# A bias ahead of a wait, a token copy ahead of a table load, and a second output buffer in a selective-scan and mixture-of-experts kernel

## The chip, the core and the metric

The kernel runs on one core of a Trainium2 chip. The metric is the time of one execution on the device, in microseconds (us). The engines are named as the profile does: PE (TensorE, matrix products), DVE (VectorE), ACT (ScalarE, activation functions), POOL (GpSimd) and SP (SyncE, which only issues transfers here). Each engine runs its own queue of instructions in order and waits on semaphores for the others.

## What is computed

The input is x of 8 batches of 512 tokens of 256 numbers. With xn the normalised x, the output is x + attention part(xn) + expert part(xn):

```python
# attention part: a selective state-space layer, 16 states per channel
x_ssm, x_gate = split(xn @ in_proj_w.T + in_proj_b)
x_conv = silu(conv4(x_ssm) + conv_b)
B, C   = split(x_conv @ bc_w.T + bc_b)
dt     = softplus(x_conv @ dt_w.T + dt_b)
h_t    = h_(t-1) * exp(dt_t * A) + dt_t * B_t * x_t      # scan over 512 tokens
y      = (sum over states of h_t * C_t + x_t * D) * silu(x_gate)
attn   = layernorm(y @ out_w.T + out_b + xn) * ln_g + ln_b
# expert part: 8 experts, the best 2 for each token
logits = silu(xn @ rw1 + rb1) @ rw2 + rb2
w      = softmax over the two largest logits
ffn    = xn + sum over the 2 experts of w_e * (silu(xn @ we1[e] + be1[e]) @ we2[e] + be2[e])
```

## The kernel before

A first block normalises x, writes the residual and computes the router's logits. A table of 71 tiles of 128 token slots is then made, each tile belonging to one expert. The main block interleaves two jobs. For each of 8 batches `b` it runs steps `i` of 0 to 8, and each step works on one expert tile `s = 9 b + i` and, in the first eight steps, on two of the sixteen states (`g = 16 b + 2 i + r`).

*The scan.* For each state DVE multiplies by B (L920), scans (L927) and multiplies by C into a ring of four (L934). POOL adds the ring into `y` (L593). ACT makes the decays `exp(dt * A)` (L757, `decay`), two instructions for each state, up to four states ahead. For the next batch the work is spread over the steps: PE projects (`proj_in`, `proj_bc`, `proj_dt`, L1126), ACT evicts (`conv_in`, `conv_act`, `bc_in`, `dt_in`), DVE applies three taps per half (L901, in steps 2 and 3), SP stores B and C to DRAM behind the loads of step 5 (L528), and ACT's `dt_in` of step 6 waits for that store. `exp_dt` and `ln_dt` follow in steps 6 and 7. In step 8, which has no scan, DVE computes `dtt` and `u` (L909, L912), and ACT makes the first two decays of the next batch. For the batch before, `proj_out` (L1148, L1151) runs on PE in steps 8 and 0, DVE adds and takes statistics (L947, L952) in steps 0 and 1, ACT and POOL normalise in steps 3 and 4, and POOL adds into `out` (L630).

*The experts.* POOL gathers a tile's tokens (L573) three tiles ahead. PE turns them (`turn_x`, L1160) into bank `up0`, and ACT copies them to `xgt` (`copy_x`, L764). PE computes `up` in two halves, banks `up0` and `up1`: each begins with a matmul that writes the bias (L1174) and goes on with 16 matmul passes (L1180). ACT applies silu (`hidden`, L791), PE computes `down` in two halves (L1190, L1194), ACT multiplies by the row's weight into `yo` (`weigh`, L799), and POOL scatters the rows with an add into `out` (L582), each scatter after the one before has landed.

In step `s` PE does: `up` half 0 of tile s+1, a projection, `up` half 1 of s+1, `down` half 0 of s, `turn_x` of s+2, `down` half 1 of s. ACT does, in step `s`:

```python
decay(b, i + 1, 0)
table_of(ACT.Silu); hidden(s + 1, 0); hidden(s + 1, 1)
...                       # evictions of this step's projections
table_of(ACT.Exp)
copy_x(s + 2)
decay(b, i + 1, 1)        # step 8: the two first states of batch b + 1
weigh(s)
```

`table_of` (L784) runs a tiny activation, so that the load of the function's table stands there in the queue. There are no projections between `hidden` and the table load in steps 7 and 8, and in the last batch only those of steps 0 and 1.

Of the kernel before, what the change touches and what calls it, by code (L numbers as in the profile page):

```python
# [6 lines left out]
ACT = mybir.ActivationFunctionType  # L7
# [5 lines left out]
P = 128  # L13
B, L, D = 8, 512, 256
# [9 lines left out]
MT = TOPK * TOK // P + E - 1  # L24
# [3 lines left out]
PARTS = 96  # L28
# [29 lines left out]
def build(nc, x, cols, rows, wmix, wroute, brows, we1, we2, consts, constb, out):  # L58
    ctx = ExitStack()
    with ctx:  # L60
        def sb(name, shape, dt=F32):
            return ctx.enter_context(nc.sbuf_tensor(name, shape, dt))

        def sem(name):
            return ctx.enter_context(nc.semaphore(name))

        psum = {n: ctx.enter_context(nc.psum_tensor("ps_" + n, [P, 512], F32))
                for n in ("up0", "up1", "yx", "fr")}
# [17 lines left out]
        sel = sb("sel", [PARTS, 32], BF16)  # L86
# [3 lines left out]
        sid = sb("sid", [P, MC], I32)  # L90
        wslot = sb("wslot", [P, MC])
# [19 lines left out]
        th = rep[:, 1, :, :].rearrange("p r l -> p (r l)")  # L111
        ht = sb("ht", [P, HBUF, KH, P])
        bup = bpart[:, 0:H].rearrange("p (e c) -> p e c", c=P)
        yo = sb("yo", [P, D])

        rt_i = sb("rt_i", [P, TB], I32)
        scrap = sb("scrap", [P, 4])
# [352 lines left out]
        s_hidden = sem("s_hidden")  # L470
        s_down_ready = sem("s_down_ready")
        s_weighed = sem("s_weighed")
        s_scattered = sem("s_scattered")
# [5 lines left out]
        yx_y, tr_x = psum["yx"][:, 0:D], psum["up0"][:, 0:D]  # L479
# [13 lines left out]
        def positive(n):  # L493
            return not isinstance(n, int) or n > 0

        with nc.Block() as block:
# [71 lines left out]
            def _(pool):  # L568
# [7 lines left out]
                def scatter(s, b, i):  # L576
                    if s > 0:
                        pool.wait_ge(s_scattered, s * 16)
                    if i == 5:
                        pool.wait_ge(s_out_rows, (b + B) * 16)  # L580
                    pool.wait_ge(s_weighed, s + 1)
                    pool.indirect_dma_start(out[:, :], bass.IndirectOffsetOnAxis(ap=sid[:, s:s + 1], axis=0), yo[:, :], None,  # L582
                                            bounds_check=TOK - 1, oob_is_err=False,
                                            compute_op=ALU.add).then_inc(s_scattered, 16)

# [94 lines left out]
            def _(act):  # L680
# [79 lines left out]
                def copy_x(j):  # L760
                    act.wait_ge(s_x_turned, j + 1)
                    if positive(j):
                        act.wait_ge(s_up_ready, j * 2)
                    act.activation(xgt[:, :, :], tr_x.rearrange("p (k c) -> p k c", k=KD), ACT.Copy).then_inc(s_x_copied, 1)  # L764
# [14 lines left out]
                def table_of(func):  # L779

                    n = tables[0]
                    if n >= 4:
                        act.wait_ge(s_table, n - 3)
                    act.activation(scrap[:, n % 4:n % 4 + 1], col[:, 0:1], func).then_inc(s_table, 1)  # L784
                    tables[0] += 1
# [8 lines left out]

                def weigh(j):
                    act.wait_ge(s_down_ready, j + 1)
                    if positive(j):
                        act.wait_ge(s_scattered, j * 16)
                    act.activation(yo[:, :], yx_y, ACT.Copy, scale=wslot[:, bass.ds(j, 1)]).then_inc(s_weighed, 1)  # L799

                def seed_root(b):
                    act.wait_ge(s_ln_eps, b + 1)
                    act.activation(rt_l[:, :], mv[:, :, 1], ACT.Ln).then_inc(s_ln_log, 1)
# [11 lines left out]
                def step(b, i):  # L815
                    s = b * STEPS + i
                    prepare = b < B - 1
                    if i + 1 < IN:
                        decay(b, i + 1, 0)
                    if i == 7 and prepare:  # L820
                        ln_dt(b + 1)
                    if s + 1 < MT:
                        table_of(ACT.Silu)
                        for h in range(2):
                            hidden(s + 1, h)
                    if i in (0, 1):
                        gate_in(b, i, front["gate", b, i])
                    if i == 0 and b > 0:
                        start_sum(b)
                    if i in (2, 3) and prepare:  # L830
                        conv_in(b + 1, i - 2, front["in", b + 1, i - 2])
                    if i == 4 and prepare:
                        conv_act(b + 1)
                    if i == 5 and prepare:
                        bc_in(b + 1, front["bc", b + 1, 0])
                        dt_in(b + 1, 0, front["dt", b + 1, 0])
                    if i == 6 and prepare:
                        dt_in(b + 1, 1, front["dt", b + 1, 1])
                    if i == 3 and b > 0:
                        seed_root(b - 1)  # L840
                    table_of(ACT.Exp)
                    if i == 3 and b > 0:
                        seed_exp(b - 1)
                    if s + 2 < MT:
                        copy_x(s + 2)
                    if i + 1 < IN:
                        decay(b, i + 1, 1)
                    if i == 8 and prepare:
                        for r in range(NU):
                            decay(b + 1, 0, r)  # L850
                    if s < MT:
                        weigh(s)
                    if i == 4 and b > 0:
                        normalise(b - 1)
                    if i == 6 and prepare:
                        exp_dt(b + 1)
# [263 lines left out]
            def _(pe):  # L1120
# [44 lines left out]

                def up(b, i, e, h):
                    j, q = b * STEPS + i, i % WBUF
                    if h == 0:
                        pe.wait_ge(s_x_copied, j + 1)
                        pe.wait_ge(s_w1[q], b * (16 * STEPS // WBUF) + 16 * (i // WBUF) + 16)  # L1170
                    if positive(j):
                        pe.wait_ge(s_hidden, j * 2 - 1 + h)
                    bank = psum[f"up{h}"]
                    pe.matmul(bank[:, :], bup[:, bass.ds(e, 1), :],  # L1174
                              sel[:, 4 * h:4 * h + 4].unsqueeze(2).to_broadcast([PARTS, 4, P]),
                              start=True, stop=False)
                    for c in range(4):
                        at = (4 * h + c) * P
                        for k in range(KD):
                            mm = pe.matmul(bank[:, c * P:(c + 1) * P], w1s[:, q, k, at:at + P], xgt[:, k, :],  # L1180
                                           start=False, stop=(c == 3 and k == KD - 1))
                    mm.then_inc(s_up_ready, 1)
# [15 lines left out]
                def step(b, i, e, e_next):  # L1198
# [3 lines left out]
                    if s + 1 < MT:  # L1202
                        up(b, i + 1, e_next, 0)
# [54 lines left out]
                e = expert(0)  # L1258
# [5 lines left out]
                for b in range(B):  # L1264
                    for i in range(STEPS):
                        e, e_next = step(b, i, e, e_next)
# [62 lines left out]
```

## Time and profile before

| | |
|---|---|
| median of 3 runs | 939.42 us (939.33 to 946.33) |
| profiled execution, its own time | 945.95 us |
| its span, first to last instruction | 944.1 us |
| mean granted clock of PE | 0.948 |

The profile is of one execution. Its span is what the rows of the trace add up to; about 1.9 us lie around it. The median of the other runs is 6.5 us below the profiled one. In the rows, L757 is line 757; "x16" is a count; `[2.36 <-ACT xgt L764]` says that the engine stood idle for 2.36 us before it and what released it. A matmul's end is modelled. PEld is PE's weight load.

### The profile page before, as it was taken

To read this page: it belongs to the slowest core of one execution; us is meant where nothing else is said; L and a number is where in the kernel's file an instruction comes from. 1 tells how busy PE (TensorE), PEld (TensorE's weight loads), DVE (VectorE), ACT (ScalarE), POOL (GpSimd) and SP (SyncE) were. 2 spreads that over 40 slices of the span, in tenths; PEclk is the share of its full clock that TensorE was granted. 3 is DMA by queue.
4 is the path that set the end of the run, shared out by engine and by line. 5 is a ranking of instruction groups with operands and counts; after the bars stand their busy time and mean duration, and the time that the engine had idled before them with its cause. 6 is when DMAs were issued, how large, how long until landed. Compare 5 with 4: busy or idle time off the path is not lost.

```text
span 944.1 us, 14375 instructions
## 1 busy us (share of the span) xinstructions
PE 796.2 (84%) x4533; PEld 637.8 (68%) x4533; DVE 786.6 (83%) x772; ACT 663.5 (70%) x1132; POOL 602.8 (64%) x384
## 2 busy tenths in 40 slices
PE   3995759978997999889988999989988998899841
PEld 2671558857786777777876887677767776778731
DVE  7818677799889988998899798989897989879973
ACT  1433577867788868876887879787887688769910
POOL 3570434657477757876777756875678478759760
PEclk9996679999999999999999999999999999999975
DMA  9945584567566876696668765887588667877721
GB/s 300 375 145 172 179 292 167 166 200 251 185 206 218 249 231 192 201 290 209 204 201 254 245 222 172 244 253 221 162 230 273 208 191 209 255 230 215 213 62 23
DMA packets 81912, 201.02 MB, mean 213 GB/s; under 512 B 7920, under 2 KB 41200, under 8 KB 81712
## 3 DMA queue, kind: packets, MB, share of 16 engines
q1 hardware_dynamic: 61424, 171.46, 53.4%
q0 software_dynamic: 19152, 26.59, 14.6%
q10 hardware_dynamic: 1264, 2.05, 0.7%
q8 instruction: 40, 0.66, 0.3%
q14 instruction: 32, 0.26, 0.1%
HBM read 174.38 MB, written 26.61 MB: 213 GB/s over the span
## 4 chain that ended last, share of the span: by engine, by line
PE 33%; DVE 26%; issue 11%; ACT 10%; DMA 8%; POOL 2%; SPq 2%; DVEq 0%; POOLq 0%; ACTq 0%
PE ps_up L1180 13%; DVE ps_drive L927 10%; PE ps_yx L1194 8%; DVE ring L934 7%; PE ps_fr L1126 6%; DMA bc_scratch<-sp 5%; DVE ps_drive L920 5%; ACT L784 3%; PE ps_fr L1151 2%; ACT da L757 2%; PE ps_up L1174 2%; DVE xx L901 2%; POOL y L593 1%; SPq L520 1%; DMA out<-yo,sid 1%
## 5 line engine op out<-in xcount | busy, mean ns | idle before, releaser
L593 POOL TENSOR_TENSOR y<-y,ring 128x1024 f32<-128x1024 f32 x127 | 328.4, 2586 | 57.8 <-ACT y L748 50.7
L927 DVE TENSOR_TENSOR_SCAN ps_drive<-da,ps_drive 128x1024 f32<-128x1024 f32 x128 | 293.7, 2295 | 48.8 <-ACT da L757 45.2
L1180 PEld LDWEIGHTS ps_up<-xgt,w1s 128*128 128x128 f32 x2272 | 285.7, 197 | 18.0 <-issue 9.6
L1180 PE MATMUL ps_up<-xgt,w1s 128*128 128x128 f32 x2272 | 285.5, 280 | 0.0
L1194 PE MATMUL ps_yx<-w,ht 128*128 x1136 | 269.8, 381 | 0.0
L1194 PEld LDWEIGHTS ps_yx<-w,ht 128*128 128x128 f32 x1136 | 205.8, 191 | 28.5 <-issue 5.0
L582 POOL DMA_INDIRECT out<-yo,sid x71 | 117.3, 1652 | 144.7 <-ACT yo L799 105.2
L784 ACT ACT_TABLE_LOAD x143 | 183.5, 1283 | 2.6
L757 ACT ACTIVATE da<-gd,col 128x511 f32<-128x511 f32 x256 | 168.4, 710 | 0.0
L920 DVE TENSOR_TENSOR ps_drive<-ps_u,rep 128x1024 f32<-128x1024 f32 x128 | 157.4, 1229 | 9.7 <-DVE ring L934 0.5
L934 DVE TENSOR_TENSOR ring<-ps_drive,rep 128x1024 f32<-128x1024 f32 x128 | 156.5, 1223 | 3.9
L791 ACT ACTIVATE ht<-ps_up 128x512 f32<-128x512 f32 x142 | 81.5, 588 | 94.5 <-PE ps_up L1180 94.4
L1126 PE MATMUL ps_fr<-xx,wm 128*128 128x512 f32 (+1 forms) x224 | 115.5, 641 | 21.5 <-ACT sp L719 9.8
L1174 PE MATMUL ps_up<-sel,bpart 96*128 96x512 bf16 x142 | 55.6, 392 | 46.9 <-ACT xgt L764 32.1
L573 POOL DMA_INDIRECT xg<-xn_scratch,gid x71 | 74.7, 1052 | 29.2 <-issue 12.7
L1126 PEld LDWEIGHTS ps_fr<-xx,wm 128*128 128x128 f32 (+1 forms) x224 | 38.1, 188 | 61.0 <-issue 36.3
L901 DVE SCALAR_TENSOR_TENSOR xx<-xs,col,xx 128x512 f32<-128x512 f32 x48 | 46.2, 962 | 24.5 <-ACT xx L697 23.9
L1174 PEld LDWEIGHTS ps_up<-sel,bpart 96*128 x142 | 14.1, 99 | 75.6 <-issue 74.6
L799 ACT ACTIVATE yo<-ps_yx,wslot 128x256 f32<-128x256 f32 x71 | 32.9, 464 | 27.0 <-DMA out<-yo,sid 25.3
L1160 PE MATMUL ps_up<-ident,xg 128*128 128x128 f32 x142 | 27.6, 276 | 13.1 <-DMA xg<-xn_scratch,gid 8.3
L727 ACT ACTIVATE sp<-ps_fr,col 128x512 f32<-128x512 f32 x16 | 11.0, 687 | 38.2 <-PE ps_fr L1126 22.3
L1151 PE MATMUL ps_fr<-wm,y 128*128 128x256 f32 x128 | 35.6, 410 | 0.0
(142 smaller groups left out, 706.5 us busy)
## 6 DMA issues: line engine op xcount, KB each, us to landing
w1s<-in_we SPq DMA_DIRECT2D x71, 1024.0 KB, 7.2
rep<-bc_scratch SPq DMA_DIRECT2D x128, 512.0 KB, 4.6
w<-in_we SPq DMA_DIRECT2D x8, 1024.0 KB, 8.9
w<-in_x SPq DMA_DIRECT2D x8, 512.0 KB, 11.0
xn_scratch<-da SPq DMA_DIRECT2D x8, 512.0 KB, 7.1
xnt_scratch<-xx SPq DMA_DIRECT2D x8, 512.0 KB, 6.6
out<-w POOLq DMA_DIRECT2D x8, 512.0 KB, 6.5
xx<-xnt_scratch SPq DMA_DIRECT2D x8, 512.0 KB, 3.6
```

The source lines that it names most:

```text
L582: pool.indirect_dma_start(out[:, :], bass.IndirectOffsetOnAxis(ap=sid[:, s:s + 1], axis=0), yo[:, :], None, bounds_check=TOK - 1, oob_is_e ...
L593: pool.tensor_tensor(y[:, :, :], y[:, :, :], ring[:, g % RING, :, :], ALU.add).then_inc(s_sum, 1)
L757: act.activation(da[:, g % DECAYS, k, 1:], dtt[:, k, 1:], ACT.Exp, scale=aneg[:, k, n:n + 1]).then_inc(s_decay, 1)
L784: act.activation(scrap[:, n % 4:n % 4 + 1], col[:, 0:1], func).then_inc(s_table, 1)
L791: act.activation(ht[:, j % HBUF, 4 * h:4 * h + 4, :], psum[f"up{h}"][:, :].rearrange("p (k c) -> p k c", c=P), ACT.Silu).then_inc(s_hidden, 1)
L920: dve.tensor_tensor(drive[:, :, :], u[:, :, :], rep[:, g % REPS, 0:1, :].to_broadcast([P, KD, L]), ALU.mult).then_inc(s_times_b, 1)
L927: dve.tensor_tensor_scan(states, da[:, g % DECAYS, :, :].rearrange("p k l -> p (k l)"), states, 0.0, ALU.mult, ALU.add).then_inc(s_scanned, 1)
L934: dve.tensor_tensor(ring[:, g % RING, :, :], drive[:, :, :], rep[:, g % REPS, 1:2, :].to_broadcast([P, KD, L]), ALU.mult).then_inc(s_times ...
L1126: mm = pe.matmul(psum["fr"][0:rows_out, :], wm[:, k, at:at + rows_out], src[:, k, :], start=(k == 0), stop=(k == KD - 1))
L1174: pe.matmul(bank[:, :], bup[:, bass.ds(e, 1), :], sel[:, 4 * h:4 * h + 4].unsqueeze(2).to_broadcast([PARTS, 4, P]), start=True, stop=False)
L1180: mm = pe.matmul(bank[:, c * P:(c + 1) * P], w1s[:, q, k, at:at + P], xgt[:, k, :], start=False, stop=(c == 3 and k == KD - 1))
L1194: mm = pe.matmul(yx_y, ht[:, j % HBUF, k, :], w2[:, bass.ds(e, 1), k, :], start=False, stop=(k == KH - 1))
```

## The change

Three edits. (1) In `up`, the bias of bank `up1` is written at the very start of the tile, in front of the wait for the token copy and of half 0; the bias of `up0` stays behind that wait, since the turned tokens lie in `up0`, but stands in front of the wait for the weights. (2) In ACT's step the token copy of tile s+2 goes in front of `table_of(ACT.Exp)`. (3) `yo` gets two buffers: `weigh(j)` waits for the scatter of tile j-2 instead of j-1.

```diff
-        yo = sb("yo", [P, D])
+        yo = sb("yo", [P, 2, D])
...
-                    pool.indirect_dma_start(out[:, :], ..., yo[:, :], None,
+                    pool.indirect_dma_start(out[:, :], ..., yo[:, s % 2, :], None,
...
                 def weigh(j):
                     act.wait_ge(s_down_ready, j + 1)
-                    if positive(j):
-                        act.wait_ge(s_scattered, j * 16)
-                    act.activation(yo[:, :], yx_y, ACT.Copy, scale=wslot[:, bass.ds(j, 1)]).then_inc(s_weighed, 1)
+                    if j > 1:
+                        act.wait_ge(s_scattered, (j - 1) * 16)
+                    act.activation(yo[:, j % 2, :], yx_y, ACT.Copy, scale=wslot[:, bass.ds(j, 1)]).then_inc(s_weighed, 1)
...
+                    if s + 2 < MT:
+                        copy_x(s + 2)
                     table_of(ACT.Exp)
                     if i == 3 and b > 0:
                         seed_exp(b - 1)
-                    if s + 2 < MT:
-                        copy_x(s + 2)
                     if i + 1 < IN:
                         decay(b, i + 1, 1)
...
                 def up(b, i, e, h):
                     j, q = b * STEPS + i, i % WBUF
+                    bank = psum[f"up{h}"]
+
+                    def bias(half):
+                        if positive(j):
+                            pe.wait_ge(s_hidden, j * 2 - 1 + half)
+                        pe.matmul(psum[f"up{half}"][:, :], bup[:, bass.ds(e, 1), :],
+                                  sel[:, 4 * half:4 * half + 4].unsqueeze(2).to_broadcast([PARTS, 4, P]),
+                                  start=True, stop=False)
+
                     if h == 0:
+                        bias(1)
                         pe.wait_ge(s_x_copied, j + 1)
+                        bias(0)
                         pe.wait_ge(s_w1[q], b * (16 * STEPS // WBUF) + 16 * (i // WBUF) + 16)
-                    if positive(j):
-                        pe.wait_ge(s_hidden, j * 2 - 1 + h)
-                    bank = psum[f"up{h}"]
-                    pe.matmul(bank[:, :], bup[:, bass.ds(e, 1), :],
-                              sel[:, 4 * h:4 * h + 4].unsqueeze(2).to_broadcast([PARTS, 4, P]),
-                              start=True, stop=False)
```

## Rows read from the trace of the kernel before

**Rows 1.** The page, part 1: busy time, share of span, instructions.
```profile
PE 796.2 (84%) x4533; PEld 637.8 (68%) x4533; DVE 786.6 (83%) x772; ACT 663.5 (70%) x1132; POOL 602.8 (64%) x384
```

**Rows 2.** Chain of waits, a batch boundary: start us, us, what.
```profile
606.27 6.54 DMA bc_scratch<-sp
...
622.27 0.59 ACT ht L791
...
633.59 2.31 DVE ps_drive L927
...
639.21 0.27 PE ps_fr L1148
```

**Rows 3.** The waits: who for whom, us in total, times, longest us.
```profile
ACT yo L799 <- DMA out<-yo,sid: 25.3, 15, 5.9
PE ps_up L1174 <- ACT xgt L764: 32.1, 25, 3.3
PE ps_up L1160 <- ACT ht L791: 4.8, 6, 0.9
DVE ps_drive L927 <- ACT da L757: 45.2, 17, 7.2
DVE xx L901 <- ACT xx L697: 23.9, 9, 5.1
```

**Rows 4.** Timeline of ACT: start us, us, engine, line, operation, at two boundaries.
```profile
425.79 1.06 ACT L791 ACTIVATE ht<-ps_up 128x512 f32<-128x512 f32 x2
...
630.09 1.28 ACT L784 ACT_TABLE_LOAD   x1
...
631.53 0.38 ACT L764 ACTIVATE xgt<-ps_up 128x256 f32<-128x256 f32 x1
631.82 2.55 ACT L757 ACTIVATE da<-gd,col 128x511 f32<-128x511 f32 x4
636.18 0.47 ACT L799 ACTIVATE yo<-ps_yx,wslot 128x256 f32<-128x256 f32 x1 [1.82 <-DMA out<-yo,sid]
```

**Rows 5.** Timeline of PE, the same boundary, from step 6 on.
```profile
616.10 0.39 PE L1174 MATMUL ps_up<-sel,bpart 96*128 96x512 bf16 x1 [2.36 <-ACT xgt L764]
616.32 1.95 PE L1180 MATMUL ps_up<-xgt,w1s 128*128 128x128 f32 x16
...
623.00 0.41 PE L1160 MATMUL ps_up<-ident,xg 128*128 128x128 f32 x2 [0.88 <-ACT ht L791]
...
625.26 0.39 PE L1174 MATMUL ps_up<-sel,bpart 96*128 96x512 bf16 x1
...
631.12 0.38 PE L1160 MATMUL ps_up<-ident,xg 128*128 128x128 f32 x2
```

**Rows 6.** Timeline of PE, the boundary at 437 us.
```profile
419.61 0.39 PE L1174 MATMUL ps_up<-sel,bpart 96*128 96x512 bf16 x1 [2.37 <-ACT xgt L764]
419.83 3.48 PE L1180 MATMUL ps_up<-xgt,w1s 128*128 128x128 f32 x16
...
427.09 0.38 PE L1160 MATMUL ps_up<-ident,xg 128*128 128x128 f32 x2
...
429.04 0.38 PE L1174 MATMUL ps_up<-sel,bpart 96*128 96x512 bf16 x1
```

**Rows 7.** Windows: us, busy per engine, PE's granted clock, DMA share, GB/s.
```profile
419.50:423.00 3.50, 3.39 (x17) 3.37 (x18) 3.36 (x3) 3.48 (x5) 1.34 (x3) 0.57 0.93 322
```

**Rows 8.** Timeline of PE, the first two tiles.
```profile
138.00 0.61 PE L1174 MATMUL ps_up<-sel,bpart 96*128 96x512 bf16 x1 [0.62 <-ACT xgt L764]
...
145.84 0.39 PE L1174 MATMUL ps_up<-sel,bpart 96*128 96x512 bf16 x1 [0.83 <-ACT xgt L764]
```

**Rows 9.** Timelines of ACT and POOL in the last batch.
```profile
862.31 0.38 ACT L764 ACTIVATE xgt<-ps_up 128x256 f32<-128x256 f32 x1
...
874.50 1.61 POOL L582 DMA_INDIRECT out<-yo,sid  x1 [1.07 <-ACT yo L799]
...
904.28 0.47 ACT L799 ACTIVATE yo<-ps_yx,wslot 128x256 f32<-128x256 f32 x1 [5.90 <-DMA out<-yo,sid]
```

More of the change, by code:

```diff
@@ L581, in scatter @@
                     pool.wait_ge(s_weighed, s + 1)
-                    pool.indirect_dma_start(out[:, :], bass.IndirectOffsetOnAxis(ap=sid[:, s:s + 1], axis=0), yo[:, :], None,
+                    pool.indirect_dma_start(out[:, :], bass.IndirectOffsetOnAxis(ap=sid[:, s:s + 1], axis=0), yo[:, s % 2, :], None,
                                             bounds_check=TOK - 1, oob_is_err=False,
```

## Prediction

> **What bounds the kernel now.** I read the totals first [rows 1]: TensorE (PE) and VectorE (DVE) are both busy over 80% of the span, so neither is a bound by itself and the order of waits has to say which one counts where. Then the chain of waits in order of time, over one batch boundary (batch 4 to 5; six others repeat it, at scans 240, 339, 437, 536, 732 and 831 us) [rows 2]. The reader is to see that one loop through all engines sets the period of a batch, 98 to 99 us:
>
> - In the middle of a batch DVE sets the pace. It runs its scans without a gap until the store of B and C for the next batch is issued (606.27). Its landing lets ScalarE (ACT) run dt_in, tables, softplus and the hidden of the last-but-one tile.
> - That hidden (622.27) releases the turn of the tokens at 623.00. From there PE is without a gap worth the name: rest of down, up of the batch's last tile, half a down, next turn at 631.12 [rows 5].
> - ACT has waited for that up. It loads the exponential's table at 630.09 and decays the first state of the next batch at 631.82 [rows 4]. DVE has waited for this decay: over the span 45.2 us in 17 waits [rows 3], seven of them at boundaries.
> - The scan then releases the layer norm's first add, which releases proj_out on PE (639.21), and PE runs without a gap through two tiles to the conv projection, which ACT hands to DVE's taps (23.9 us of waits in nine, about 3 at each batch [rows 3]). Then DVE sets the pace again.
>
> So a microsecond added in front of the decay at 631.82 is paid once per boundary, seven times. What happens to PE between the taps and the store of B and C costs or brings nothing: DVE is the late one there.
>
> **Part 1, the bias of the second bank in front of the wait.** Nothing is added or removed: 71 matmuls change place. Where PE waits for the token copy (25 waits, 32.1 us [rows 3]), this one, 0.2 to 0.4 us [rows 5], is now done inside the wait. Its own wait (the hidden of that bank one tile earlier) is met, since ACT runs that hidden ahead of the copy that PE waits for. On the loop PE waits for no token copy but a short one at 625.26, so per batch only one place gains: in step 0 the bias stood behind proj_out's wait for the norm's add. There the next projection waits for DVE's second add almost as long, and I take 0.1 us per boundary: -0.7. The start is different: PE waits 0.62 and 0.83 us for the first two copies [rows 8], and from there the chain is PE's. One bias in each wait, 0.4 and 0.2 us: -0.6.
>
> **Part 2, the copy in front of the table load.** ACT does the same three things, in another order. Before, at the boundary, the load (630.09) lay beside the half down and the turn on PE, and the copy came at 631.53, just when the turn (631.12, about 0.4 us) was done; the decay came 0.29 us after the copy [rows 4, 5]. Now ACT, a strict queue, stands at the copy until the turn is done, and only then loads the table. From the copy's start to the decay's it takes: copy 0.38 (the load does not overlap it), load to the next instruction's start 1.44 less about 0.03 of wait for the turn, so 1.79 to 1.8. That is 1.5 us more than 0.29.
>
> Against it stands what PE gains. In step 6 the copy comes 1.4 us sooner, and PE starts that tile 1.6 us sooner instead of at 616.10. But the next turn already waited 0.88 us for ACT's hidden in five of the seven boundaries (623.00; the sixth such wait is in the last batch [rows 3, 5]), and that hidden sits behind a softplus and three tables on ACT. So the 1.6 us become a longer wait for the hidden, 2.5 to 2.6 us, and nothing reaches the decay. The hidden itself comes 0.12 later, for the copy no longer overlaps its neighbours. The next copy is early: turn to next bias is 2.26 us there (623.00 to 625.26) and 1.95 where no copy is waited for (427.09 to 429.04) [rows 5, 6], a gain of 0.3, net 0.15. So the decay moves by 1.5 - 0.15 = +1.36 us at five boundaries. At the other two (437 and 536) PE ran up of this tile slowly (16 matmuls 3.48 us instead of 1.95) and its turn, 427.09, waited for nothing [rows 6]. ACT's hidden for it ran from 425.79 and takes 0.59 [rows 2, 4]; with the 0.12 and 0.1 to the turn PE can start it at 426.6. So the earlier start is worth 0.47 here, and the decay moves by 1.5 - 0.47 = +1.04. Sum: 5 x 1.36 + 2 x 1.04 = +8.9.
>
> In other steps a delay of up to 1.5 us (where nothing stands between hidden and copy) falls on decays for which DVE isn't waiting: of the 17 waits, the ten away from the boundaries are three of the first batch and seven of 0.6 us in step 1, ahead of the 3 us in which DVE waits for the taps anyway. What hides it is the scan in hand, with its products before and behind. If that cover were gone, it would cost 1.5 us in about three steps of each batch, 31 us. The copy is earlier by 1.4 us in steps 2 to 4 and 6, where PE did wait for it, and all that ends in DVE's stretch. In the last batch no projections stand between hidden and copy: the copy of step 2 (862.31) was already held by the turn. Its table now pushes two decays, the next hidden and so the weighing whose end POOL waits for at 874.50 [rows 9]; from there POOL has no gap up to the last accumulation into out, which holds the end. +1.0.
>
> What does a table cost? The load is 1.28 us and the next instruction starts 1.44 us after the load starts [rows 4]. The Trainium skill (ScalarE: Activation LUTs, What ACT_TABLE_LOAD costs) gives the same 1283 ns for the load but adds a drain of about 1380 ns to every switch, 2.66 us. By that the load exposed at each boundary would cost some 1.2 us more, and the sum would be some 8.5 us higher. No drain of that size stands behind the loads of this trace.
>
> **Part 3, two buffers for weighted rows.** It takes away ACT's wait for the scatter: 15 waits, 25.3 us [rows 3]. Seven of them stand right after the boundary's decays (0.6 to 1.8 us, as at 636.18 [rows 4]). Behind them are a decay for the third scan and a hidden that waits for PE anyway, and the delay of part 2 eats up most of the wait itself. The longest two are in the tail, the first 5.9 us [rows 9]; POOL is late there, with scatters and sums queued in order, not ACT. Scatters still wait for each other. I take 0; the bound on the good side is all 25.3.
>
> **The clock of PE.** Six of the seven boundaries have a long wait for the copy of step 6. After two of them the granted clock fell to half, 1.2 GHz (0.57 mean over 419.5 to 423 [rows 7]). The wait of 2.37 us was followed by it [rows 6], the one of 2.36 [rows 5] and the longest, 3.3 [rows 3], were not, so I can't say beforehand which will be. There it cost little, for the hidden behind it was late anyway. The change shortens that wait to 1 us and makes one of 2.6 us right in front of the turn, where the loop runs through PE. A fall to half there costs 3.48 - 1.95 = 1.5 us on sixteen matmuls and 0.1 on the next, 1.6 us [rows 5, 6]. I take two of them as before: +3.3. Ends: none, and six, +9.8. The Trainium skill (TensorE: Matmul & The Clock Gate, What's actually happening) says that the throttled state is the default and activity releases it; the two falls behind waits agree.
>
> **Sum.** -0.6 -0.7 +8.9 +1.0 +0 +3.3 = +11.9 us. The profiled execution took 945.95 us (span 944.1), so it would take 957.9. It is 6.5 us above the median of the runs, 939.42; none of the terms hangs on that difference that I can see, so I add them to the median: 951.3.
>
> **Rivals.**
> - *No low clock* (0.22): the longer wait before the turn never meets a fall of the clock. 939.4 + 8.6 = 948.0, at the edge of what can be told.
> - *Every such wait meets it* (0.05): 939.4 + 8.6 + 9.8 = 957.8.
> - *The second buffer pays* (0.13): ACT's wait for the scatter after the boundary's decays, and in the tail, was on a path that the chain does not show. If all 25.3 us count, 951.3 - 25.3 = 926.0; it decides for faster from about 21 us on. For it: the waits of more than 5 us in the tail, with PE's last downs behind them. Against it: no piece of the chain is a wait of ACT's weighing for a scatter.
> - *The copy's advance reaches the decay* (0.10): not ACT's hidden but PE sets the turn at all boundaries, as it does at 437 and 536. Then 1.4 to 1.6 us of advance pay for the 1.5 of the load at each, and with the start's gain it is 939.4 - 0.6 - 0.7 - 0 to 1 = 937 to 938. Against it: five waits of 0.88 us of the turn for the hidden.
> - The forecast itself: 0.50.
>
> **How the numbers follow.** A measurement of this kernel tells about 1% from no change, so the bounds are 930.0 and 948.8. Slower: the forecast 0.50, every wait 0.05, and 0.05 of the case at 948.0: 0.60. Faster: half of the second buffer's 0.13 and a little of the copy's advance: 0.08. The same: 0.32. The range reaches down to the copy's advance and leaves out most of the second buffer's case below and the far end of the clock above, less than 2 in 10: 937 to 957. The forecast's own range is 948.8 to 955.
>
> **What would show it.** After the change: at a boundary ACT's copy stands after a wait for the turn (1 us or more), with the table load behind it, and DVE's first scan of a batch waits over 1 us longer for its decay than before, up to 8.5 where it was 7.2; L927's wait for decays grows from 45 to 55 us or more. PE's waits for the copy fall from 32 us to about half, and its waits for hidden in front of the turn grow from 4.8 to 15 or more. ACT's waits for the scatter are gone. The first tap of batch 1 comes 0.6 us sooner. Wrong, if the period between first scans does not grow by 1 us, if the decays wait in the middle of batches too (then it is dearer), or if the tail after 890 us gets shorter, which would be the second buffer's doing.

## The result, and the profile after

The changed kernel takes 963.8 us (median of 6 runs, 959.5 to 968.2), the kernel before 940.2 on the same chips (6 runs). The ratio is 1.0219, with a 95% interval of 1.0182 to 1.0255: 20.6 us slower. (The medians lie 23.6 us apart; the ratio also weighs a run of 953.3 us of the kernel before.) The prediction was 951.3, in a range of 937 to 957, and the measured time lies above that range. Its sign was right; by the ratio its sum, +11.9, was 8.7 us short.
Against [rows 1] the busy time of the page moved by 4.6 us on PE and 6.7 on DVE, and so most of the 19 us are waits. Time at half clock counts as busy:

```profile
PE 800.8 (83%) x4533; PEld 637.5 (66%) x4533; DVE 793.3 (82%) x772; ACT 666.8 (69%) x1132; POOL 603.1 (63%) x384
```

The waits of the changed kernel (who for whom, us in total, times, longest us). Its `up` is at L1173 and L1185, its `down` at L1195 and L1199.

```profile
DVE ps_drive L927 <- ACT da L757: 63.0, 17, 11.9
ACT xgt L764 <- PE ps_up L1160: 32.1, 28, 4.2
PE ps_up L1160 <- ACT ht L791: 18.3, 10, 2.7
PE ps_fr L1148 <- DVE xtok L947: 16.9, 7, 3.2
ACT yo L799 <- DMA out<-yo,sid: 6.0, 1, 6.0
PE ps_up L1173 <- ACT xgt L764: 1.7, 2, 1.0
PE ps_up L1185 <- DMA w1s<-in_we: 27.8, 14, 3.5
```

Against [rows 3]: DVE's waits for decays grew from 45.2 to 63.0 us and PE's waits for the hidden in front of the turn from 4.8 to 18.3. PE's waits for the copy (32.1) and ACT's for the scatter (25.3) are all but gone. So the three edits do what they say. What PE waited for the copy, ACT now waits for the turn (32.1), and PE waits 27.8 us for weights in front of L1185; no line of the kernel before names weights, but its bias stood behind the wait for them, and there it has 14.2 us in 8 waits without a releaser. The fourth line is the one to look at: PE's wait in front of `proj_out` for the norm's add, not among the rows of the prediction, was this before:

```profile
PE ps_fr L1148 <- DVE xtok L947: 10.5, 8, 1.7
```

**A boundary with the clock at full.** Timeline of ACT after, batch 2 to 3 (start us, us, engine, line, operation, idle before it and its releaser), to set beside [rows 4, 5]:

```profile
433.85 0.60 ACT L791 ACTIVATE ht<-ps_up 128x512 f32<-128x512 f32 x1 [1.19 <-PE ps_up L1185]
435.91 0.38 ACT L764 ACTIVATE xgt<-ps_up 128x256 f32<-128x256 f32 x1 [1.46 <-PE ps_up L1160]
436.31 1.28 ACT L784 ACT_TABLE_LOAD   x1
437.60 0.20 ACT L784 ACTIVATE scrap<-col 128x1 f32<-128x1 f32 x1
437.71 2.54 ACT L757 ACTIVATE da<-gd,col 128x511 f32<-128x511 f32 x4
```

And PE over the same stretch, the turns of steps 7 and 8:

```profile
427.67 0.41 PE L1160 MATMUL ps_up<-ident,xg 128*128 128x128 f32 x2 [1.87 <-ACT ht L791]
...
435.49 0.38 PE L1160 MATMUL ps_up<-ident,xg 128*128 128x128 f32 x2
```

ACT idles 1.46 us in front of the copy, and only then does the load begin. From PE's last turn to the first decay it is 437.71 - 435.49 = 2.22 us; before, 631.82 - 631.12 = 0.70. That is the exposed load, +1.52 us, and the same at all seven boundaries within 0.06. From step 7's turn to step 8's it is 7.82 us, before 8.12 (631.12 - 623.00): 0.30 given back, so +1.22 net. That holds at the five boundaries where the turn had waited 0.88 before. At the two where it had waited for nothing (427.09 and 525.74), turn to turn was 7.80 already, but `dt_in` (L727) to the turn was 10.68 us there and is 10.10 everywhere now: 0.56 given back in all, so +0.96 net. The hidden comes late enough to eat the rest of PE's earlier start, as the wait of 1.87 shows.

**Half clock behind step 7's turn.** Timeline of PE after, batch 4 to 5:

```profile
630.17 0.41 PE L1160 MATMUL ps_up<-ident,xg 128*128 128x128 f32 x2 [2.70 <-ACT ht L791]
630.41 2.81 PE L1199 MATMUL ps_yx<-w,ht 128*128 x8
633.02 1.06 PE L1173 MATMUL ps_up<-sel,bpart 96*128 96x512 bf16 x2
633.87 4.11 PE L1185 MATMUL ps_up<-xgt,w1s 128*128 128x128 f32 x32
...
639.66 0.38 PE L1160 MATMUL ps_up<-ident,xg 128*128 128x128 f32 x2
```

Turn to turn is 9.49 us instead of 7.82: +1.67. This happened at three boundaries (after 326.8, 527.5 and 630.2 us), each behind a wait of 2.70. A fourth wait of that size, and one of 2.53, were not followed by it.

**Half clock behind step 0's wait.** The same happens in front of `proj_out`. Timeline of PE after, in a batch with the clock at full (444.75) and in one without (649.28):

```profile
444.75 0.27 PE L1148 MATMUL ps_fr<-bpart,sel 96*128 96x256 bf16 x1 [2.40 <-DVE xtok L947]
444.86 1.03 PE L1151 MATMUL ps_fr<-wm,y 128*128 128x256 f32 x4
...
649.28 0.37 PE L1148 MATMUL ps_fr<-bpart,sel 96*128 96x256 bf16 x1 [3.17 <-DVE xtok L947]
649.45 1.91 PE L1151 MATMUL ps_fr<-wm,y 128*128 128x256 f32 x4
651.15 0.42 PE L1148 MATMUL ps_fr<-bpart,sel 96*128 96x256 bf16 x1
651.37 1.91 PE L1151 MATMUL ps_fr<-wm,y 128*128 128x256 f32 x4
653.08 2.93 PE L1185 MATMUL ps_up<-xgt,w1s 128*128 128x128 f32 x16
```

Windows of the clean boundary and of this stretch (us, busy per engine, PE's granted clock, DMA share, GB/s):

```profile
427.80:437.50 9.70, 9.70 (x63) 8.53 (x62) 6.34 (x4) 6.70 (x11) 8.94 (x5) 1.00 0.82 255
649.20:656.00 6.80, 6.72 (x27) 5.81 (x28) 6.01 (x5) 0.00 (x0) 0.00 (x0) 0.56 0.46 150
```

Timeline of DVE, the first tap (L901) of each of the two batches, whose first scans start at 439.13 and 643.65:

```profile
471.88 2.86 DVE L901 SCALAR_TENSOR_TENSOR xx<-xs,col,xx 128x512 f32<-128x512 f32 x1 [2.75 <-ACT xx L697]
...
678.90 2.87 DVE L901 SCALAR_TENSOR_TENSOR xx<-xs,col,xx 128x512 f32<-128x512 f32 x1 [2.75 <-ACT xx L697]
```

The decay is later, so the scan, DVE's work behind it and the add are later, while PE has the same work as before: its wait grew from 1.5 us to 2.4 and more. In the stretch behind the wait of 3.17 the granted clock is 0.56, near the 1.2 GHz level. It fell behind a wait of 2.83 (546.25) too, and in the batch from 751.93 behind one of 2.71 for POOL's `y` in step 8's `proj_out` (753.10), but not behind one of 2.82 (345.58). Here PE leads up to the taps: from step 0's `proj_out` to the first tap it is 27.13 us in the clean batch and 29.62 in the other, and the first tap stands 32.75 us behind the first scan in the clean batch and 35.25 in the other. (DVE's own wait, 2.75, is the same in both, because on the way its scans had stood longer for PE and for a decay.) In three batches the tap was late, by 1.16, 2.50 and 1.07 us; before in none. It is the same in all the kernels of this study: of 78 batches between the second and the eighth first scan, 14 have a late first tap (by 1.07 to 2.84 us), and exactly these 14 have half clock between their first scan and that tap.

**A chain through POOL's queue.** The batch that began at 643.65 took 108.3 us. PE waited 3.48 us for weights in it and then ran `up` at a low clock (32 passes are 3.73 us at full):

```profile
694.10 6.40 PE L1185 MATMUL ps_up<-xgt,w1s 128*128 128x128 f32 x32 [3.48 <-DMA w1s<-in_we]
```

Its chain of waits (start us, us, what):

```profile
706.95 1.61 POOL out L582
708.55 2.39 POOL y L593
710.95 2.31 POOL xtok L624
713.30 2.74 issue
716.05 11.89 DMA out<-xtok
...
728.79 0.20 POOL out L582
...
736.55 9.31 DMA out<-yo,sid
...
746.67 1.57 POOL out L582
748.24 2.38 POOL y L593
```

The scatter of step 4 left late (706.95, 63.3 us behind the first scan, where 57.5 to 58.7 is usual), the sum into `out` waited for its landing, the next scatter for the sum's (7.59 us of idle POOL), and the gathers queued behind it came late for the turns. That boundary's wait for the decay is the 11.9 of the list above.

So the trace gives, over the six batches between first scans 2 and 8, 615.3 us against 590.9: +24.4. By stretches: first scan to first tap +4.7, all of it the three late taps; first tap to `dt_in` (L727) +3.5; `dt_in` to step 8's turn +7.0; turn to first scan +9.2, the exposed load. In the third stretch, 2.3 us were given back by the order, 3 x 1.67 = 5.0 are the slow turns and 4.2 the chain's batch; with its share of the second stretch the chain comes to about 6. The rest of the second stretch, about 1.6 us over five batches, is not explained by any run. The part of the trace ahead of the six batches is 2.8 shorter (first batch's first scan at 132.51 instead of 134.78, and 0.5 of the first period), the one behind them 2.3 shorter (110.50 for 112.75).

### The profile page after: what moved, and what is told of

Read it like the earlier page. It is cut to its first block, busy times and chain, and to the rows that moved or that the text cites. A ratio compares the mean times of both kernels' runs of the same rounds, so it can differ in the third digit from the quotient of the medians.

```text
span 963.4 us, 14373 instructions
## 1 busy us (share of the span) xinstructions
PE 800.8 (83%) x4533; PEld 637.5 (66%) x4533; DVE 793.3 (82%) x772; ACT 666.8 (69%) x1132; POOL 603.1 (63%) x384
## 4 chain that ended last, share of the span: by engine, by line
PE 27%; DVE 22%; DMA 14%; issue 13%; ACT 8%; POOL 7%; SPq 0%; POOLq 0%; DVEq 0%; ACTq 0%
PE ps_up L1185 9%; PE ps_yx L1199 8%; DVE ps_drive L927 7%; DMA out<-yo,sid 7%; DVE ring L934 6%; PE ps_fr L1126 5%; DMA out<-xtok 5%; DVE ps_drive L920 4%; POOL y L593 3%; ACT L784 2%; ACT da L757 2%; DVE xx L901 2%; PE ps_fr L1151 2%; POOL xtok L624 1%; PE ps_up L1173 1%
## 5 line engine op out<-in xcount | busy, mean ns | idle before, releaser
L593 POOL TENSOR_TENSOR y<-y,ring 128x1024 f32<-128x1024 f32 x127 | 324.5, 2555 | 76.7 <-ACT y L748 64.1
L1185 PEld LDWEIGHTS ps_up<-xgt,w1s 128*128 128x128 f32 x2272 | 279.7, 198 | 58.6 <-DMA w1s<-in_we 33.7
L1185 PE MATMUL ps_up<-xgt,w1s 128*128 128x128 f32 x2272 | 283.3, 282 | 27.8 <-DMA w1s<-in_we 27.8
L1199 PE MATMUL ps_yx<-w,ht 128*128 x1136 | 271.9, 383 | 0.0
L1199 PEld LDWEIGHTS ps_yx<-w,ht 128*128 128x128 f32 x1136 | 206.7, 192 | 29.1 <-issue 5.3
L582 POOL DMA_INDIRECT out<-yo,sid x71 | 119.7, 1686 | 151.3 <-ACT yo L799 97.7
L1126 PE MATMUL ps_fr<-xx,wm 128*128 128x512 f32 (+1 forms) x224 | 113.4, 631 | 22.6 <-ACT sp L719 10.3
L901 DVE SCALAR_TENSOR_TENSOR xx<-xs,col,xx 128x512 f32<-128x512 f32 x48 | 52.6, 1095 | 24.2 <-ACT xx L697 23.6
L1160 PE MATMUL ps_up<-ident,xg 128*128 128x128 f32 x142 | 27.9, 278 | 30.7 <-ACT ht L791 18.3
L764 ACT ACTIVATE xgt<-ps_up 128x256 f32<-128x256 f32 x71 | 27.1, 382 | 33.5 <-PE ps_up L1160 32.1
L1173 PE MATMUL ps_up<-sel,bpart 96*128 96x512 bf16 x142 | 46.3, 398 | 2.8 <-ACT xgt L764 1.7
L1160 PEld LDWEIGHTS ps_up<-ident,xg 128*128 128x128 f32 x142 | 19.0, 142 | 41.5 <-issue 22.0
L1148 PE MATMUL ps_fr<-bpart,sel 96*128 96x256 bf16 x32 | 9.7, 302 | 34.7 <-DVE xtok L947 16.9
```

What stands on the lines that cost most here:

```text
L593: pool.tensor_tensor(y[:, :, :], y[:, :, :], ring[:, g % RING, :, :], ALU.add).then_inc(s_sum, 1)
L1126: mm = pe.matmul(psum["fr"][0:rows_out, :], wm[:, k, at:at + rows_out], src[:, k, :], start=(k == 0), stop=(k == KD - 1))
L1199: mm = pe.matmul(yx_y, ht[:, j % HBUF, k, :], w2[:, bass.ds(e, 1), k, :], start=False, stop=(k == KH - 1))
```

## Experiments

Eleven kernels, each in 10 runs (e2, e7 and e9 in 4, e11 in 12), beside the kernel before on the same chip (941.8 to 943.1 us there, 23 to 25 runs). Ratios have their 95% interval. "Six batches" is the time between the second and the eighth first scan of the one profiled execution; before it is 590.9, after 615.3.

| label | us | ratio | six batches |
|---|---|---|---|
| e1_bias_only | 938.7 | 0.9958 [0.9932, 0.9983] | 589.6 |
| e2_copy_only | 962.1 | 1.0225 [1.0173, 1.0277] | 606.6 |
| e3_two_yo_only | 941.0 | 0.9983 [0.9951, 1.0015] | 590.9 |
| e8_bias_and_yo | 939.3 | 0.9963 [0.9933, 0.9992] | 586.1 |
| e6_not_steps_6_8 | 942.3 | 1.0014 [0.9981, 1.0047] | 592.8 |
| e4_not_step8 | 944.4 | 1.0018 [0.9990, 1.0046] | 597.1 |
| e7_only_step8 | 960.8 | 1.0176 [1.0104, 1.0247] | 613.6 |
| e5_fill_waits | 954.9 | 1.0117 [1.0084, 1.0150] | 605.8 |
| e9_fill_step0 | 955.4 | 1.0121 [1.0078, 1.0164] | 603.9 |
| e10_step8_filled | 950.0 | 1.0083 [1.0052, 1.0115] | 599.4 |
| e11_late_softplus | 938.1 | 0.9946 [0.9921, 0.9971] | 583.1 |

### Each part alone

e1 is the kernel before with the `up` of the change, e2 with its order of copy and table, e3 with its two buffers. Each diff is the part with its number (1, 2, 3) of the diff in the section on the change.

> The kernel before with part 1 alone, the bias of the second bank ahead of the wait for the token copy. Theory (the cost is made by the copy in front of the table load): no cost here, a gain of about 1 us, 937 to 940 us, and the turn of step 7 still waits 0.9 us or so for ACT's hidden. Rival (the earlier bias lets PE run ahead and idle longer before its next wait, so that its clock falls in the places that set the end): 945 us or more, with more low stretches of the granted clock than the four of before between 238 and 831 us.

> The kernel before with part 2 alone, the token copy ahead of the exponential's table load in every step. Theory (this part makes the cost): 955 to 964 us, each boundary's turn to first scan 1.5 us longer (3.6 instead of 2.1 us), PE's wait for the hidden in step 7 over 1.8 us. Rival (the low clock needs the bias in front as well): 948 to 950 us, the seven exposed loads alone, 7 x 1.2 = 8.5 us above before, with no low stretch between the turn of step 7 and the first scan.

> The kernel before with part 3 alone, two buffers for the weighted rows. Theory: ACT's 25 us of waits for scatters go to under 7 and nothing of it reaches the end, 939 us within 0.3%. Rival (the tail, which is 2.3 us shorter after the change, is shorter because of the second buffer): 937 us, the stretch from the last batch's first scan to the end under 111 us instead of 112.8.

The whole cost is part 2's: e2 alone has the ratio of the whole change. Part 1 gains 4 us by the ratio (I had 1.3). Part 3 gives nothing that the ratio can tell, though its stretch from the last first scan to the end was 110.4 us instead of 112.8, the sign that the rival had named. From the waits of e3: ACT's wait for the scatter fell from 25.3 us to one wait in the tail, and the six batches stayed as they were:

```profile
ACT yo L799 <- DMA out<-yo,sid: 5.5, 1, 5.5
```

The same view of e2: step 0's wait had grown without the other parts:

```profile
PE ps_fr L1148 <- DVE xtok L947: 20.0, 8, 3.0
```

### Parts 1 and 3 together

The whole change without its part 2.

> The change without part 2 at all: bias ahead of the wait and two buffers for the weighted rows. Theory: the gain of the bias (0.4%) and nothing or 0.2% of the second buffer: 937 to 939 us. Rival (both together let PE run ahead of DVE into longer waits): 943 us or more.

939.3 us, the base from which part 2 is taken apart below.

### Which step's copy costs

The whole change, with the copy left behind the table load in some steps (e4: 8; e6: 6 and 8), and the kernel before with the copy moved in step 8 alone (e7). Shown for e4:

```diff
-                    if s + 2 < MT:
+                    if s + 2 < MT and i != 8:            # e6: i not in (6, 8); e7: i == 8
                         copy_x(s + 2)
                     table_of(ACT.Exp)
                     if i == 3 and b > 0:
                         seed_exp(b - 1)
+                    if s + 2 < MT and i == 8:            # e6: i in (6, 8); e7: i != 8
+                        copy_x(s + 2)
```

> The whole change, but in step 8 of each batch the token copy stays behind the table load. Theory (the load exposed at the boundary is a price of its own, 1.5 us in each of seven): turn to first scan back at 2.1 us, total 10.6 us under the change, about 953 us, the rest being low clock. Rival (the low clock is nearly all, and the load at the boundary is hidden by other waits): 961 us or more.

> The whole change, but the token copy stays behind the table load in steps 6 and 8. Theory (the early copy of step 6 only moves PE's idle time in front of step 7's turn, where the half clock falls on the loop): the turn's wait back to 0.9 us and turn to turn at 8.1 us or less at every boundary, 3 to 5 us under the variant that leaves out step 8 alone (944.4), so about 940 us. Rival (step 6's early copy is harmless, and low stretches come from somewhere else): 944 us again.

> The kernel before with one thing: in step 8 alone the token copy goes in front of the table load. Theory: 1.5 us at each of seven boundaries, and with the longer wait of PE for the norm's add in step 0 the low stretches behind it, three or so of 1 to 2.5 us each: 943 + 10.5 + 4.5 = 955 to 960 us. Rival (step 0's low clock needs PE to run ahead by the early copies): 951 to 954 us and no first tap later than 32.8 us after the first scan.

Left behind in step 8 alone, the copy gives back 19 us of the 20.6 (ratio 1.0018), and moved there alone it costs 17 (1.0176, a wide interval). One instruction in one of nine steps is the case. For e4 I had expected 953 us, 10.6 less than the change and the rest left as half clock; it was 944.4. The half clock of step 0 went with the load: with the decay on time step 0's wait was 0.4 to 1.7 us and all six taps stood at 32.75. e6 and e4 have the same ratio, where I had expected e6 to be 3 to 5 us faster, so the early copy of step 6 costs nothing that can be told, though e4's profile shows the slow turn at three boundaries and e6's at none: step 7's wait for the hidden was 2.7 us at most in e4, 1.2 in e6. In e7 the waits of step 0 were 2.9 to 3.3 us and the first tap was late in all six batches, by 1.5 to 2.8 us.

### Keeping PE's clock

e5 is the whole change with matmuls that add zeros, 8 in front of step 0's `proj_out` and 16 in front of step 7's turn. e9 has only those in step 0. e10 has part 1, the copy of step 8 alone and the filler of step 0. What is computed is the same in all three.

```diff
                     if i == 0 and b > 0:
+                        for _ in range(8):
+                            pe.matmul(psum["up1"][:, :], bup[:, bass.ds(e_next, 1), :],
+                                      sel[:, 28:32].unsqueeze(2).to_broadcast([PARTS, 4, P]),
+                                      start=False, stop=False)
                         proj_out(b - 1, 1)
...
                         down(s, e, 0)
+                        if i == 7:                       # e5 alone
+                            for _ in range(16):
+                                pe.matmul(yx_y, sel[:, 31:32].to_broadcast([PARTS, P]), bpart[:, H:BW],
+                                          start=False, stop=False)
                         if s + 2 < MT:
                             turn_x(s + 2)
```

> The whole change, and in its two long waits of PE on the loop it now multiplies by zero rows: 16 short matmuls that add zero to the half-done down in front of step 7's turn, 8 that add zero to the second up bank in front of step 0's proj_out. The result is the same numbers. Theory (beside the exposed load, 1.5 us at each boundary, the cost is the half clock that follows these waits, 3 x 1.7 behind the turn and 4.7 behind proj_out, with what the latest of them drags along): no low stretch in these places, turn of step 7 to next turn 7.8 us at every boundary, first tap 32.8 us after the first scan in every batch, 950 to 954 us. Rival (the clock is a by-product and the time goes to late decays and POOL): 960 us or more, with the periods of the batches as after the change.

> The whole change with PE's filler (8 matmuls that add zeros) only in step 0, in front of proj_out's wait for the norm's add, and none in front of step 7's turn. Theory (the half clock behind step 0's wait makes the first tap late and, in one batch, starts a chain through POOL's queue): all first taps stand 32.75 us behind the first scan, turn to turn stays 9.5 us at about three boundaries, and the time lies between that of the change (963.8) and that with both fillers (954.9), nearer to the latter: 956 to 958. Rival (step 7's half clock is what costs): the time stays at 961 to 964. Second rival (the filler itself delays the add's projection): the taps come later than 33.5 us everywhere.

> Bias ahead (part 1), the copy in front of the table load in step 8 alone, one buffer yo, and the filler in step 0. The same step-8 copy without part 1 and without filler took 960.8 us with taps late in all six batches. Theory (that cost is 1.5 us of table load at each of seven boundaries plus the half clock in step 0): with the clock held only the table load is left, 938.7 (part 1 alone) + 7 x 1.4 = 948.5 us, periods 98.5 to 99.7, taps at 32.75. Rival (the load in front of the decay costs more by another path, such as the later scans pushing every store and gather): 955 us or more with taps at 32.75.

Timeline of PE in e9, step 0 of batch 5, whose first scan is at 640.85:

```profile
643.56 1.91 PE L1211 MATMUL ps_up<-sel,bpart 96*128 96x512 bf16 x8
646.48 0.27 PE L1148 MATMUL ps_fr<-bpart,sel 96*128 96x256 bf16 x1 [1.01 <-DVE xtok L947]
646.58 1.03 PE L1151 MATMUL ps_fr<-wm,y 128*128 128x256 f32 x4
```

The add comes no sooner, PE has 1.9 us more to do, and it takes 9.2 us off the whole change (1.0219 to 1.0121; the two intervals make that good to about 5). In e5, e9 and e10 all 18 first taps of the six batches stand at 32.75. The filler was not put into the kernel before; its trace has no late tap that it could mend. e5 and e9 come out the same, so it is step 0's filler that pays; the 16 matmuls in step 7 bring nothing that can be told on top, though e5's trace has no slow turn of 9.5 us (one of 8.67, six of 7.8). e9's expected rival, that step 7's half clock costs, falls. In e9 turn to turn was 9.5 us at two of the seven boundaries, where I had expected about three.

e10 has the exposed load and, in step 0, a held clock. ACT in it, at one boundary:

```profile
537.44 0.38 ACT L764 ACTIVATE xgt<-ps_up 128x256 f32<-128x256 f32 x1 [1.46 <-PE ps_up L1162]
537.84 1.28 ACT L784 ACT_TABLE_LOAD   x1
539.13 0.20 ACT L784 ACTIVATE scrap<-col 128x1 f32<-128x1 f32 x1
539.24 2.54 ACT L757 ACTIVATE da<-gd,col 128x511 f32<-128x511 f32 x4
```

It took 950.0 us where 948.5 was expected and the rival said 955 or more. From e1, the same without the copy's move and the filler, it is 0.0125 by the ratio: 11.8 us for seven boundaries, 1.7 each, with e1's and e10's intervals about 4 us to either side. In their profiles the six batches differ by 599.4 - 589.6 = 9.8, 1.6 each. The load of 1.5 is most of it or all.

### A version that takes work off the boundary

Parts 1 and 3, and the softplus of the next batch's dt moved behind step 7's copy:

```diff
-                    if i == 7 and prepare:
-                        ln_dt(b + 1)
...
-                    if i == 6 and prepare:
-                        exp_dt(b + 1)
...
+                    if i == 7 and prepare:
+                        exp_dt(b + 1)
+                        ln_dt(b + 1)
                     if s < MT:
                         weigh(s)
```

> Parts 1 and 3 without part 2, and on ACT the next batch's exp_dt and ln_dt moved from steps 6 and 7 (in front of step 7's hidden) to behind step 7's token copy, so that the hidden that releases the turn of step 7 comes about 3 us sooner. Theory (at the boundary the turn waits 1.0 to 1.2 us for that hidden, and PE sets the rest up to the decay): the turn comes about 1 us sooner, but the two tables and 2.1 us of softplus then stand in front of step 8's hidden, which gives part back; 0.3 to 1.0 us per boundary, 932 to 937 us. Rival (ACT is the bound of step 7, not the order in it): the hidden of step 8 comes late by as much, and the time stays at 939 to 942.

Timeline of PE in it, batch 4 to 5, the turns of steps 7 and 8, and then DVE's first scan:

```profile
611.39 0.38 PE L1159 MATMUL ps_up<-ident,xg 128*128 128x128 f32 x2
...
619.19 0.38 PE L1159 MATMUL ps_up<-ident,xg 128*128 128x128 f32 x2
```

```profile
621.82 2.30 DVE L926 TENSOR_TENSOR_SCAN ps_drive<-da,ps_drive 128x1024 f32<-128x1024 f32 x1 [2.44 <-ACT da L757]
```

Step 7's turn waits for no hidden any more, PE waits next in step 8's `proj_out` (1.9 us for POOL's `y`), and DVE's wait is 2.1 to 2.4 us, where it was at least 3.67 at the second to eighth first scans before. The six batches take 583.1, 7.8 less than before and 2.9 less than e8. In the runs it is 0.9946 [0.9921, 0.9971], 5 us faster than before; against e8 (0.9963) the intervals overlap, so what the move adds by itself isn't settled. Its median lies between the 932 to 937 of the theory and the 939 to 942 of the rival. In two of the six batches half clock stood behind the wait in step 8 (332.1 and 526.6), and the first tap was late by 1.6 us, so holding PE's clock there is still to be tried. Its profiled execution, 929.1 us, was the fastest of its twelve. It has the lowest median and ratio of this study, by less than its uncertainty.

## Why the prediction was right or wrong

By the ratios, at 942 us, the steps e8, e4, e9 and the whole change form a ladder. Each rung is the difference of two measured ratios, good to 3 to 5 us:

| what is added | from, to | measured | predicted |
|---|---|---|---|
| parts 1 and 3 | before, e8 | -3.5 | -1.3 |
| copies ahead, all steps but 8 | e8, e4 | +5.2 | 0 there, +3.3 for half clock in step 7, +1.0 tail |
| copy ahead in step 8, clock of step 0 held | e4, e9 | +9.7 | +8.9 |
| half clock behind step 0's wait | e9, whole | +9.2 | 0 |
| sum | | +20.6 | +11.9 |

- **The exposed load was right**, in size and place: 1.52 us from turn to decay against 1.5, 0.30 given back, 9.7 us against 8.9. The split into five boundaries at 1.36 and two at 1.04 was right as well: they measured 1.22 and 0.96, 8.0 us together.
- **The step that failed is the clock of PE.** I looked for a longer wait at one place, in front of step 7's turn, priced the fall there and stopped. A later decay makes every wait longer in which PE waits for what hangs on it. The next is step 0's wait for the norm's add, and I had named it myself, twice: as a place where the bias gains 0.1, and in the loop, as the point from which PE runs without a gap to the taps. It went from 1.5 to 2.4 us and more, and half clock behind it falls on PE's stretch of the loop. The sum has nothing for it; it measured 9.2 us, give or take 5, as much as the 8.7 by which the sum was short.
- **How that became 9 us** is shown in part. The profiled execution of the change is 11.4 us longer than e9's over the six batches: 4.7 are the late taps, 3.3 are two more slow turns of step 7, which step 0's filler doesn't hold, and about 3 the end of the batch with the chain through POOL's queue. The chain followed on the latest tap, and in e5, e9 and e10, with all taps on time, no batch after the first took over 103 us. But it doesn't need a late tap. In e4's batch from 631.45 the tap stands at 32.75, and behind PE's wait for weights the same chain runs, smaller:

```profile
678.84 6.71 PE L1187 MATMUL ps_up<-xgt,w1s 128*128 128x128 f32 x32 [2.92 <-DMA w1s<-in_we]
```

```profile
692.00 1.61 POOL L582 DMA_INDIRECT out<-yo,sid  x1 [3.21 <-ACT yo L799]
...
711.65 1.63 POOL L582 DMA_INDIRECT out<-yo,sid  x1 [6.25 <-DMA out<-xtok]
```

That batch took 102.7 us. So a wait for weights with half clock about it is enough to start the chain; that the late tap made it longer in the changed kernel is argued, not shown.

- **Half clock behind step 7's turn** was seen three times where I took two, at 1.67 us instead of 1.6. What it costs the kernel is open: the traces show 5.0 us on the way to the decay, and e6 against e4, and e5 against e9, show nothing above their few us of uncertainty. What the +5.2 of the other steps' copies is made of stays open too; e6 against e8 is +4.8 already (about as much as its uncertainty), with the copies of steps 6 and 8 in their old place, and I had costed the others at nothing, as covered by scans. The traces show where it lies: e6's six batches are 6.7 us longer than e8's (592.8 and 586.1), and all of it stands between first tap and `dt_in`, where the store of B and C is issued later and lands later. Why, no run shows, and none took the copies one by one.
- **Part 1's start.** The first scan came 2.3 us sooner after the change, but over the kernels it lies between 130.3 and 135.4 us with part 1 (e11 and e10) and between 131.4 and 134.8 without (e3 and before). The term of 0.6 can't be read from that.
- **Part 3 and the tail.** In the batches part 3 was right at 0, and the longest wait, 5.9 us, is in the tail and stayed there (6.0). But from the last first scan to the end it is 110.4 to 112.4 us in the eight kernels with two buffers and 112.6 to 114.0 in the five with one. So the second buffer seems to be worth about 2 us in the tail, where the prediction had nothing; its last sentence had named a shorter tail as a sign of being wrong. e3's ratio (-1.6 us, give or take 3) doesn't settle it. The +1.0 for the copy's part in the tail is too small to see: 110.5 after, 110.4 in e3. Its reason was misread, too: before, POOL stands idle 6.01 us at 900.92 and 16.47 us at 933.10, ahead of the last accumulation, which waits for DVE.
- **The rivals.** "No low clock" (948.0) is best met by e5, the whole change with PE kept busy in both waits: +11.0 us by the ratio, give or take 3, where the rival had +8.6. "Every such wait meets it" (957.8) fell short too, for it looked at the same wrong place. "The second buffer pays" falls with e3, "the copy's advance reaches the decay" with the wait of 1.87 us for the hidden.
- **The drain** behind a table load. The Trainium skill (ScalarE: Activation LUTs, What ACT_TABLE_LOAD costs) makes a switch 2.66 us with it. The trace doesn't agree: from the load at 436.31 to the decay it is 1.40 us.

## What to carry to other kernels

When a step on the loop comes later by a known amount, don't price that alone: list every wait of the tensor engine for what hangs on it, add the delay to each, and price the half clock behind each by what the engine does next. A table load that stands in front of a wait costs nothing while the wait lasts; put a waiting instruction ahead of it and its 1.3 us, here 1.5 with what the order adds, are laid bare, once for each time that the wait was on the loop. Where a wait has grown, a few matmuls that add zeros ahead of it are a cheap way to find out whether it is the wait or the clock behind it that costs.

## What was not expected of the hardware

- Eight matmuls that add zeros, 1.9 us of work in gaps of 2.4 to 3.2, bring 9.2 us, give or take 5 (1.0219 to 1.0121). Without them the granted clock was 0.56 over 6.8 us in one batch. The Trainium skill (TensorE: Matmul & The Clock Gate, What's actually happening) says that the throttled state is the default and activity releases it; the runs agree, with these numbers.
- Waits of equal length are not equal in what follows: of four waits of 2.70 us in front of step 7's turn after the change, three were followed by half clock (turn to turn 9.5 us) and one was not (7.8); in e9 one of 2.34 and one of 2.70 were, and another of 2.70 was not.
- Half clock outlasts the wait: from 649.28 it held through the ten matmuls of `proj_out` and into the `up` behind them (2.93 us for 16 instead of 1.95).
